# Second stage of a fused adaLN + attention + MoE kernel: the modulation on VectorE, x loaded straight into the rows, one more row field, biases inside ScalarE's copies, norms one slot nearer to their use

## What is computed

```python
    h = _layernorm(x, axis=-1) * (1 + cb) + sb
    x = x + gb * _L0_ffn_ref(h, ...)

    def _mha(x, Wqkv, bqkv, Wo, bo):      # 4 heads; attends over the 16 sequences, per token
        ...
        return o @ Wo.T + bo
    def _moe(x, Wg, W1, b1, W2, b2):
        logits = xf @ Wg.T
        idx = jnp.argmax(logits, axis=-1)
        for e in range(E):                # E = 8 experts, DF = 512
            m = (idx == e)[:, None].astype(xf.dtype)
            h = jax.nn.relu(xf @ W1[e] + b1[e])
            out = out + m * (h @ W2[e] + b2[e])
    y = _layer_norm(x + _mha(x, ...), g1, be1)
    z = _layer_norm(y + _moe(y, ...), g2, be2)   # the ffn's result
```

## Time and profile before

| | us |
|---|---|
| median of 3 runs | 1309.68 |
| lowest, highest | 1306.42, 1319.79 |
| the profiled execution: device time | 1320.8 |
| its span in the trace | 1318.9 |
| first stage, to about | 829 |
| second stage, slot by slot | 829 to about 1104 |
| third stage, to | 1319 |

### The profile page before, as it was taken

How to read it: one execution, slowest core, us unless ns; L and a number is a source line. 1 busy time by engine, 2 the same in 40 slices (tenths; PEclk the granted TensorE clock), 3 DMA queues, 4 the chain that set the end, 5 groups by cost and what they waited for, 6 DMA issues and landing times. The chain is left out here.

```text
span 1318.9 us, 50557 instructions
## 1 busy us (share of the span) xinstructions
PE 1155.9 (88%) x18130; PEld 981.3 (74%) x18130; DVE 868.0 (66%) x3982; ACT 937.4 (71%) x3446; POOL 912.2 (69%) x738
## 2 busy tenths in 40 slices
PE   4899999999999999999999999378899771888882
PEld 2688888888888888888888888256777561877772
DVE  6778778778778678777777663245675562466573
ACT  3788988988988988988988988356566430544551
POOL 3677777777777777777777765676778563367675
PEclk9999999999999999999999999688788865989996
DMA  5766666656666666666666673131222125643200
GB/s 178 199 163 166 163 151 163 166 144 167 166 152 163 167 150 162 161 154 164 166 147 155 157 194 92 49 115 37 89 91 79 63 74 166 169 131 108 63 28 25
DMA packets 102454, 174.67 MB, mean 132 GB/s; under 512 B 19118, under 2 KB 55729, under 8 KB 102080
## 3 DMA queue, kind: packets, MB, share of 16 engines
q1 hardware_dynamic: 95232, 153.82, 45.4%
q0 software_dynamic: 6400, 16.82, 3.5%
q10 hardware_dynamic: 576, 0.79, 0.2%
HBM read 31.86 MB, written 24.68 MB: 43 GB/s over the span
## 5 line engine op out<-in xcount | busy, mean ns | idle before, releaser
L548 POOL TENSOR_TENSOR qk<-mm,sw 128x1024 f32<-128x1024 f32 x128 | 304.2, 2377 | 122.4 <-DMA sw<-mm 122.2
L632 ACT ACTIVATE pr<-sm,mn 128x96 f32<-128x96 f32 x1024 | 371.3, 374 | 0.3 <-DVE mn L468 0.3
L456 DVE TENSOR_TENSOR mm<-bank,cos 128x512 f32<-128x512 f32 x256 | 175.5, 686 | 172.5 <-PE bank L306 165.2
L554 POOL TENSOR_TENSOR pr<-pr,ri 128x768 f32<-128x768 f32 x128 | 188.2, 1471 | 74.5 <-DVE ri L477 73.0
L632 ACT ACTIVATION_READ_ACCUMULATOR pr<-sm,mn 128x1 f32 x1024 | 204.9, 200 | 0.0
L468 DVE CUSTOM_DVE_ANT_0 sm<-bank,msk 128x96 f32<-128x96 f32 x1024 | 192.1, 253 | 5.3 <-PE bank L330 5.3
L457 DVE TENSOR_TENSOR mm<-bank,sin 128x512 f32<-128x512 f32 x256 | 174.3, 681 | 0.0
L346 PE MATMUL bank<-pT,vw 96*64 96x64 f32 x4096 | 147.5, 225 | 0.0
L316 PEld LDWEIGHTS bank<-wo,ot 128*128 128x128 f32 x1024 | 133.4, 191 | 14.3 <-ACT ot L641 3.3
L1241 ACT ACTIVATE xq<-bank,b1t 128x128 f32<-128x128 f32 x288 | 81.7, 375 | 84.5 <-PE bank L1105 73.8
L346 PEld LDWEIGHTS bank<-pT,vw 96*64 96x64 f32 x4096 | 129.8, 138 | 15.2 <-issue 0.2
(11 more groups left out here) (203 smaller groups left out, 2451.4 us busy)
## 6 DMA issues: line engine op xcount, KB each, us to landing
sw<-mm SPq DMA_DIRECT2D x512, 128.0 KB, 2.3
vw<-vn SPq DMA_DIRECT2D x128, 192.0 KB, 2.5
vw<-vn SPq DMA_DIRECT2D x128, 128.0 KB, 2.3
rr<-sorted_scratch SPq DMA_DIRECT2D x72, 192.5 KB
vw<-vn SPq DMA_DIRECT2D x96, 64.0 KB, 2.2
xt<-in_x SPq DMA_DIRECT2D x16, 256.0 KB, 4.1
x_scratch<-x SPq DMA_DIRECT2D x16, 256.0 KB, 2.7
xq<-x_scratch SPq DMA_DIRECT2D x16, 256.0 KB, 2.8
```

Of the source, the lines that this page charges most:

```text
L456: dve.tensor_tensor(mm[s % 2][:, 0, j, :], PJ[u % 2][:, :], cos[:, :], ALU.mult)
L548: pool.tensor_tensor(qk[i % 2][:, :, 32:], mm[i % 2][:, 0, :, :], sw[i % 2][:, :, :], ALU.add)\
L554: pool.tensor_tensor(t, t, ri[i % 2][:, :].unsqueeze(2).to_broadcast([P, 8, WK]), ALU.mult)\
L632: ins = act.activation(pr[i % 2][:, h, p, :], ms_[i % 2][:, h, p, :], ACT.Exp, scale=-1.0, bias=mn[i % 2][:, h, p:p + 1], accum_out=sums[i ...
```

## The change

1. Rows get a fourth field: y, x, gated scale, gated shift, target row (`RW = 4 * C + 1`, 513 words, 2052 bytes instead of 1540). The two gated fields are the same for every token and are written once, for all 40 row slots of `rr`, by one DMA that SP issues behind the load of quad 2.
2. x is loaded from `x1_scratch` straight into field 1 of the rows (`quad_rows(u)[:, :, C:2 * C]`); the buffers `xq` are gone. SP's waits change with it: for u >= 3 it waits for the statistics of quad u-3, and for u >= 10 also until the four scatters of quad u-10 have landed (`s_sca`), since the row slot is reused.
3. The modulation (scale and shift on 128x512) moves from POOL to DVE, between the statistics of x and the router's argmax. POOL's add into `rr` is gone, and so is ACT's copy of the gated scale (L1151).
4. The output projection's bias: the constant `c0` and its two matmuls per quad (L1076, L1078) are gone. bo is added to `modp`'s shift, v's bias goes into ACT's copy of the attention output, and ACT's `hT` copy subtracts bo again.
5. Norms, `hc` and the modulation handle quad s+1 instead of s+2 in slot s; the statistics of x are for quad s+2 instead of s+3. The loop starts at -2 instead of -3 and ends one slot sooner.
6. In the third stage DVE adds field 3 to field 1, one 128x512 operation per quad (18 in all).

The diff, cut to its core:

```diff
-RW = 3 * C + 1
+RW = 4 * C + 1
...
-    FIRST, LAST = -3, NQ + 7
+    FIRST, LAST = -2, NQ + 6
...
             for u in range(NQ):
                 if u >= 3:
-                    sp.wait_ge(s_cn, u - 2)
-                    sp.wait_ge(s_c0, u - 2)
+                    sp.wait_ge(s_b1, 8 * (u - 2))
+                if u >= NR:
+                    sp.wait_ge(s_sca[(u - NR) % 4], 64 * ((u - NR) // 4 + 1))
+                    sp.wait_ge(s_cn, u - NR + 1)
                 src = x1_d[32 * u:32 * u + 32].rearrange("(k t) b c -> (t b) k c", k=4)
-                sp.dma_start(xq[u % 3][:, :, :], src).then_inc(s_xq[u % 3], 16)
+                sp.dma_start(quad_rows(u)[:, :, C:2 * C], src).then_inc(s_xq[u % 3], 16)
+                if u == 2:
+                    sp.wait_ge(s_po, 5)
+                    sp.dma_start(rr[:, :, 2 * C:4 * C], gg[:, :, :].rearrange("p a c -> p (a c)").unsqueeze(1)
+                                 .to_broadcast([P, 4 * NR, 2 * C])).then_inc(s_fl, 16)
...
-                u = s + 2
-                if quad(u):
-                    v = h2[u % 7][:, :, :]
-                    pool.wait_ge(s_cn, u + 1)
...
-                    pool.tensor_tensor(v, hc[u % 2][:, :, :], modp[:, C:2 * C].unsqueeze(1).to_broadcast([P, 4, C]),
-                                       ALU.mult).then_inc(s_h2, 1)
-                    if u >= NR:
-                        pool.wait_ge(s_sca[(u - NR) % 4], 64 * ((u - NR) // 4 + 1))
-                    pool.tensor_tensor(quad_rows(u)[:, :, C:2 * C], xq[u % 3][:, :, :],
-                                       gg[:, 0:1, :].to_broadcast([P, 4, C]), ALU.add).then_inc(s_c0, 1)
-                    pool.wait_ge(s_h2, 2 * u + 1)
-                    pool.tensor_tensor(v, v, modp[:, 0:C].unsqueeze(1).to_broadcast([P, 4, C]), ALU.add).then_inc(s_h2, 1)
...
-                    pe.matmul(d4, avg[:, :], c0h[:, :].unsqueeze(1).to_broadcast([P, 4, C]),
-                              start=True, stop=False, skip_group_check=True)
-                    pe.matmul(d4, avg[:, :], c0l[:, :].unsqueeze(1).to_broadcast([P, 4, C]),
-                              start=False, stop=False, skip_group_check=True)
...
+                u = s + 1
+                if quad(u):
+                    v = h2[u % 7][:, :, :]
+                    dve.wait_ge(s_cn, u + 1)
...
+                    dve.tensor_tensor(v, hc[u % 2][:, :, :], modp[:, C:2 * C].unsqueeze(1).to_broadcast([P, 4, C]),
+                                      ALU.mult).then_inc(s_h2, 1)
+                    dve.wait_ge(s_h2, 2 * u + 1)
+                    dve.wait_ge(s_do, 1)
+                    dve.tensor_tensor(v, v, modp[:, 0:C].unsqueeze(1).to_broadcast([P, 4, C]), ALU.add).then_inc(s_h2, 1)
...
+                if k == 2 and 0 <= q < NQX:
+                    x = xs[q % NX]
+                    dve.wait_ge(s_xs[q % NX], 64 * (q // NX + 1))
+                    dve.tensor_tensor(x[:, :, C:2 * C], x[:, :, C:2 * C], x[:, :, 3 * C:4 * C], ALU.add).then_inc(s_xe, 1)
```

More of the change, by code:

```diff
@@ L684, in phase2 @@
     blk_m = sbt(p2, "blkm", [P, 4, 32], BF)
-    c0 = sbt(p2, "c0", [P, C])
-    c0h = sbt(p2, "c0h", [P, C], F32R)
-    c0l = sbt(p2, "c0l", [P, C], F32R)
-    avf = sbt(p2, "avf", [P, P])
-    avg = sbt(p2, "avg", [P, P], F32R)
     trb = sbt(p2, "trb", [P, 2 * P], BF)
     nhalf = sbt(p2, "fnh", [P, 8])
-    xq = [sbt(p2, f"xq{n}", [P, 4, C]) for n in range(3)]
     hc = [sbt(p2, f"hc{n}", [P, 4, C]) for n in range(2)]
@@ L773, in quad, with norms @@
         return 0 <= v < NQ
+    def norms(s):
+        return 4 * len([v for v in range(FIRST, s + 1) if quad(v + 1) or quad(v - 4)])
     w1h = sbt(p2, "w1h", [P, NE * DF], BF)
@@ L810, in phase2 @@
     s_gx = sem("s_gx")
+    s_xe = sem("s_xe")
     s_rt = sem("s_rt")
@@ L979, in _ @@
             pe.transpose(X[0][:, 0:P], bc[:, 0, :], ident[:, :])
-            pe.transpose(X[0][:, P:2 * P], bc[:, 1, :], ident[:, :]).then_inc(s_eo, 1)
-            pe.matmul(X[1][:, 0:C], fb[:, 2:3].to_broadcast([P, P]), wfo, start=True, stop=True).then_inc(s_eo, 1)
-            pe.wait_ge(s_do, 8)
-            pe.wait_ge(s_ao, 2)
+            pe.transpose(X[0][:, P:2 * P], bc[:, 1, :], ident[:, :])
+            pe.transpose(X[0][:, 2 * P:3 * P], bc[:, 4, :], ident[:, :]).then_inc(s_eo, 1)
+            pe.wait_ge(s_do, 7)
+            pe.wait_ge(s_ao, 1)
             for s in range(FIRST, LAST):
@@ L1143, in _ @@
                     act.wait_ge(s_r, r_use[("t1", u)] + 1)
+                    if u == 0:
+                        act.wait_ge(s_ao, 1)
                     if u >= 2:
@@ L1186, in _ @@
                         .then_inc(s_ye, 1)
-                u = s + 2
+                u = s + 1
                 if quad(u) or quad(s - 4):
-                    act.wait_ge(s_ln, 4 * len([v for v in range(FIRST, s + 1) if quad(v + 2) or quad(v - 4)]))
+                    act.wait_ge(s_ln, norms(s))
                 if quad(u):
@@ L1193, in _ @@
                     for j in range(4):
-                        ins = act.activation(hc[u % 2][:, j, :], xq[u % 3][:, j, :], ACT.Identity,
+                        ins = act.activation(hc[u % 2][:, j, :], quad_rows(u)[:, j, C:2 * C], ACT.Identity,
                                              scale=rs[s % 2][:, 0, j:j + 1], bias=nb[s % 2][:, 0, j:j + 1])
@@ L1202, in _ @@
                     for j in range(4):
-                        act.activation(oT[u % 2][:, j * P:(j + 1) * P], X[j][:, 0:P], ACT.Copy).then_inc(s_oe, 1)
+                        act.activation(oT[u % 2][:, j * P:(j + 1) * P], X[j][:, 0:P], ACT.Identity, bias=fb[:, 2:3])\
+                            .then_inc(s_oe, 1)
                 u = s - 4
@@ L1257, in prepare @@
                 dve.wait_ge(s_l2, 16 * 6)
-                dve.wait_ge(s_eo, 2)
-                dve.tensor_tensor(c0[:, :], X[1][:, 0:C], bc[:, 4, :], ALU.add).then_inc(s_do, 1)
+                dve.tensor_tensor(modp[:, 0:C], modp[:, 0:C], bc[:, 4, :], ALU.add).then_inc(s_do, 1)
                 for g in range(4):
```

65 lines of the change are left out of this document (28 added, 37 removed).

## The result

The changed kernel takes 1360.4 us (median of 4 runs, 1358.3 to 1361.1), the kernel before 1312.3 beside it (1306.4 to 1319.8): a ratio of 1.036 with a 95% interval of 1.030 to 1.042. It is slower, by 48 us. The forecast was 1346 in a range of 1326 to 1366: the direction, the place and the mechanism came out as forecast, and the time was 14 us above the forecast.

What follows compares the result with a forecast made beforehand. No engine full; a loop DVE, ACT, PE, DVE sets the slot, with POOL nearly as long. +43.4 - 10 - 2 + 4 + 1 = +36.4 on the median 1309.7 gives 1346, range 1326 to 1366.

Steps and rivals of the forecast that it cites:

- The bound and the mechanism: Second stage: a DVE, ACT, PE loop; in slots 7 to 11 expert weights queue behind the same slot's scatter.
- Rivals 1 and 2: Slots 7 to 11: weights still in time, 1295, chance 0.05; or the wait costs little, 1318, chance 0.08.
- Slots 7 to 11: Second stage: late expert weights make these slots take 111.5 us instead of 68.1, +43.4, bounds +32 and +58.
- The landing: Slots 7 to 11: the scatter lands 2.1 us after its last issue, bounds 1 and 3.5.
- the ranks: Slots 7 to 11, DVE: the ranks end 6.16 us after the residual add, as in slot 10 before.
- The bound of +58: Slots 7 to 11, upper bound: landing 3.5 and q and k at half clock give 25.6 us a round.
- What it saves: Slots 4 to 15 without the waits: slots of 12.0 or 11.3 us, -10, bounds 0 and -20.
- Start: Before slot 4: one slot less and modulation on DVE, against the fill of the rows; -2, bounds -4 and +10.
- Change to the third stage: Between second and third stage: pads, scatters and row loads a third larger; +4, bounds 0 and 7.
- Third stage: Third stage: DVE's 18 added operations, 12.4 us, mostly covered by idle time; +1, without that cover 12.
- Beside 87 us of idle time: Third stage: DVE, busy 113.7 of 201 us, has idle time to cover its added 12.4 us.
- The rule weighed: Slots 7 to 11: DVE's new pair lengthens scatter issues by 0.7 us a round; by the skill page 0.

Runs made afterwards that it cites:

- the wait alone: The kernel before with one added SP wait: from quad 10 the x load waits until quad u-10's scatter has landed; 1330.1 us, ratio 1.035.
- the kernel with wide rows: The kernel before with rows of 513 words instead of 385, the added field filled by one DMA and not used; 1289.7 us, ratio 1.003.
- the weights first: The changed kernel with expert u-9's raw weights load issued ahead of the scatter wait instead of behind it; 1287.0 us, ratio 1.0007.
- the fastest kernel: The kernel before with only the two modulation operations moved from POOL to DVE, one slot ahead of use instead of two; 1270.7 us, ratio 0.988.
- biases with DVE modulation: The kernel before with the constant matmuls replaced by biases in ACT's copies and the two modulation operations moved to DVE; 1275.9 us, ratio 0.992.
- 11 row buffers: The changed kernel with 11 quads of row buffers instead of 10, SP's order untouched; 1282.9 us, ratio 0.9995.
- POOL modulation: The changed kernel with weights loads ahead of the scatter wait and the modulation pair back on POOL behind its scatters; 1333.6 us, ratio 1.039.

## Why the prediction was right, and where its sizes failed

**The bound and the mechanism: right.** The weights of a slot were asked for after the last scatter of that slot in slots 7 to 11 and not in 12; PE stood 11.2, 9.1, 12.0, 12.3 and 12.1 us before them; the granted clock fell to the 1.2 GHz level behind it; the wait alone gave the loss and its removal in two ways (order, one more buffer) took it back. Rivals 1 and 2 failed, as neither the scatter nor its issue became fast enough: ranks before the scatter, and four issues of 1 us each with 0.3 between, came out as in the sum. The five landings stood at T + 20.0 to T + 21.7, where the sum had 18.3.

**Slots 7 to 11: +43.4 forecast, +55.5 measured.** The sum was a chain of terms from one landing to the next, and slot 9 can be held against it term by term (us):

| term | forecast | slot 9 |
|---|---|---|
| weights landed to residual add | 4.0 | 3.86 |
| residual add to ranks | 6.16 | 7.73 |
| to the first scatter | 0.8 | 0.89 |
| four issues (with DVE's share) | 5.66 | 5.42 |
| last issue to the x load | 2.1 | 3.43 |
| x issue, then weights landing | 3.56 | 3.55 |
| round | 22.3 | 24.9 |

Two terms were mis-sized. The landing I set at 2.1 between 1 and 3.5, by the size of a scatter; it is 2.1 for rows of 385 words and 3.2 for the changed kernel's 513, and in slots 10 and 11 it was 3.85 and 3.55, over my upper bound. And the ranks I took at 6.16 from slot 10 of the kernel before, the shortest of its five: the other four slots have 6.90 to 7.06. Part of the difference is the ranks' product. In slot 10 of the kernel before it was over before POOL's multiplication of the probabilities began:

```profile
976.24 0.19 DVE L1315 TENSOR_TENSOR rk<-rk,oh 128x32 f32<-128x32 f32 x1
```

In slot 9 of the changed kernel, and in all five of these slots, it took 1.01 or 1.02, because that multiplication had begun 0.08 us before it and held it to its end:

```profile
970.20 1.05 POOL L915 TENSOR_TENSOR fpp<-fpp,fri 128x512 f32<-128x512 f32 x1 [1.38 <-DVE fri L1283]
```

The rest is that the scores come 0.71 us later than DVE wants them (1.22 in slot 7, none in slot 10); in slot 9 PE had just made its output projection at half clock (2.06). I had looked at this step ("about when DVE wants the scores") and rounded it to nothing. The wait of 0.70 for the exponential is no difference: it stands in slot 10 of the kernel before as well.

```profile
975.11 0.69 DVE L1301 TENSOR_REDUCE fsm<-fpp 128x16 f32<-128x512 f32 x1 [0.70 <-ACT fpp L1162]
```

Over the five slots the ranks are 8.1 us longer than in the sum, the landings 5.4, the scatter issues 2.5 shorter, and the rest 1.1 longer: together the missing 12.1. The bound of +58 came near to the result, but it was made of a landing of 3.5 and half clock on the projections of q and k, and not of these two terms.

**What it saves: -10 forecast; -9.5 measured in the two profiles** (slots 4 to 6 -7.9, 12 to 15 -1.6), and -11.3 away from the first chip (-6.4 and -4.9 against the kernel with wide rows). Only the part in slots 4 to 6 is firm. In slots 12 to 15 the first profile has two standstills of DVE:

```profile
DVE lg L1337 <- remote: 13.4, 2, 6.7
```

No profile of the other chips has a wait of this kind in the slots, and there the kernel before with the scatter wait, which has none of the helpful parts, takes 46.8 us against 45.5 of the changed one. In slots 7 to 11 the saving did not come at all: with the weights first they take 14.2 us each, where the same working gave 12.0. The parts, too, are less alike than the sum had them: moving the pair to DVE is worth 11 to 15 us over the whole kernel, and folding the biases, costed at nothing, costs 3 to 4, with an interval from 0.1 to 8.5. Whether ACT's longer copies are the reason was not shown.

**Start: -2 forecast, -4.0 measured in the two profiles,** at the edge of its bounds. The other chips are nearer to the forecast: from the end of the first stage's last copy on ACT (L641) to slot 4 it is 59.5 to 61.3 us in the three kernels there with POOL's modulation two slots ahead, and 57.8 to 59.7 in the five with the changed kernel's start, 2.1 less on average. The fill took 22.5 us from issue to landing, for 21 forecast, and no run shows a loss by it.

```profile
rr<-gg SPq DMA_DIRECT2D x1, 5120.0 KB, 22.5
```

**Change to the third stage: +4 forecast.** 5.2 away from the first chip. On the first it was 10.6 (62.1 before, 72.7 after), and what the other 5 us are was not tried. It did not come from the gap between quads 0 and 1, where I put 1.4 of it: that is 4.67 us now (1170.38 to 1175.05) after 4.2 in the earlier trace rows. The first transposes waited longer:

```profile
1170.36 1.12 PE L1076 MATMUL bank<-ident,rr 128*128 128x128 f32 x4 [29.38 <-DMA rr<-sorted_scratch]
```

**Third stage: +1 forecast, +4.1 away from the first chip** (mean of six and six). "Beside 87 us of idle time" counted idle time that was not where the add fell. In the two profiles of the first chip this stage took 201.1 us before and 188.3 after; no run elsewhere shows such a difference, and the kernel before with wide rows took 175.5 there. The profiled execution of the kernel before took 1320.8 us, 8.5 above the median of the runs; I had noted such a difference without asking in which stage it lay. So the first chip's two profiles can't size this term, and the others can. These two profiles differ by 39.7 us in all, close to the forecast's 36.4, and that is luck: a third stage 12.8 us shorter, which no part of the change explains, covers what slots 7 to 11 were short by.

**The rule weighed.** I took 0.7 us a round for scatters beside DVE, from one row. The changed kernel shows 0.5 in slots 8 and 9 and 0.15 or less in the other three, so the row's sign was right and its size smaller here. The Trainium skill (SBUF — State Buffer, section Who interferes with whom) infers that such DVE instructions leave the generation of descriptors alone; the runs speak against that, as below.

**In sum away from the first chip.** From the stage table, the changed kernel against the kernel before with wide rows, which ran on another of the three chips: slots 7 to 11 +53.6, slots 4 to 6 -6.4, slots 12 to 15 -4.9, third stage +4.2; the change to it +6.6 against the mean of the kernels with narrow rows; the start +0.9 (slot 4 at 882.9 and 882.0). Together +54.0 us, against 54.2 between the medians on the changed kernel's chip. The forecast of +36.4 is 18 us short of that: 10 of it in slots 7 to 11, about 3 each in the start, the change to the third stage and the third stage, less 1 for a saving that came out larger.

## What to carry to other kernels

In an in-order queue, look at what stands behind a new wait and in which step of the pipeline it is used; if the wait ends in the same step as the use, the queue has turned a buffer's slack into a serial chain. Moving the load ahead of the wait or one buffer more gives all of it back, and a gain of the same edit can be had alone: the two modulation operations on DVE, with nothing else changed, take 1.2% off (0.6 to 1.8). And when a loop is summed, price each step from several slots and not from one: the one slot taken here for the ranks was the shortest of five, and a step can be five times as long when another engine's operation lies beside it.

## What the runs showed of the hardware that was not expected

**A scatter issue waits for a DVE operation with two SBUF inputs.** An issue (0.97 us) that begins while such a DVE operation of 128x512 or 128x1024 runs is longer by what is left of that operation, less about 0.13. In slot 9 above it began 0.61 us before the DVE operation's end and took 1.46, 0.49 more. Beside the residual add `uu`, which has one input in PSUM, it stays at 0.97. In the fastest kernel it began 1.16 us before the end of an addition of 128x1024 and took 1.04 more:

```profile
958.11 1.22 DVE L1366 TENSOR_TENSOR b2r<-b2r,bc 128x1024 f32<-128x1024 f32 x1
```

The issue beside it:

```profile
958.17 2.01 POOL L923 DMA_INDIRECT sorted_scratch<-rr,slot  x1 [0.30 <-issue]
```

Where 0.28 was left it took 1.12 (926.50 in the changed kernel), and the row fits too: 1.05 left, 1.89. A DVE operation that begins inside a running issue does not lengthen it (the first issue of a slot stays at 1.09). It is the other way round when the two begin together. In slot 11 DVE's operation began 0.04 us before the issue; then the issue was not longer and DVE's operation was, 0.76 instead of 0.69. The traces have 14 cases in which this operation began at most 0.04 us before the issue, all alike, and from 0.05 us on the issue is the longer one. The case of slot 11:

```profile
1024.57 0.76 DVE L1317 TENSOR_TENSOR h<-h,modp 128x512 f32<-128x512 f32 x1
```

And the issue:

```profile
1024.61 0.97 POOL L925 DMA_INDIRECT sorted_scratch<-rr,slot  x1 [0.30 <-issue]
```

**A small DVE operation is held until a big POOL operation ends.** The ranks' product (L1292, 128x32, both inputs in SBUF) takes 0.18 or 0.19 us. In the fourteen traces it began 126 times beside POOL's multiplication of 128x512 (1.05 us), each time 0.08 us after it, and took 1.01 or 1.02 in all 126; in the other 98 it took 0.18 or 0.19. POOL's 128x8 step of 1.67 us beside it (L905 of the kernel before, 976.16) did not lengthen it.

**A copy of ACT with a per-partition bias costs more.** Four copies of 128x128 from PSUM take 1.10 to 1.15 us with a bias column (as `Identity`) and 0.74 to 0.79 without (as `Copy`); one of 128x512 takes 0.69 against 0.60.

**The landing of an indirect scatter is later with the longer row.** The waiting queue went on 1.9 to 2.4 us after the last issue's end for 1540 bytes a row, and 2.5 to 4.0 after it for 2052. From an issue to its own landing the median is 3.1 us in the two traces with 1540 bytes that show landings (the scatter wait in the kernel before, and biases with DVE modulation), and 4.0, 3.6 and 3.6 in the three with 2052 (weights first, 11 row buffers, POOL modulation). With 1540 bytes, from the scatter wait in the kernel before:

```profile
sorted_scratch<-rr,slot POOLq DMA_INDIRECT x64, 3.1
```

With 2052 bytes, from the weights first:

```profile
sorted_scratch<-rr,slot POOLq DMA_INDIRECT x64, 4.0
```

These kernels differ in more than the row, so the row's own share is not shown.
